# A convolution in products of 32 by 32 and an attention with the values stationary, in a four-layer network

## What is computed

```python
x = x + channel_attention(group_norm(x))             # layer 0
y = bn(einsum('bchw,oc->bohw', x, pw_w)) + x          # layer 1
x = gelu(bn(dwconv13x13(y)) + bn(y * dw1))            # 13 x 13 taps for each channel by itself
t = to_tokens(x)                                      # (16, 256, 96)
t = t + attention(ln(t))      # layer 2: 6 heads of 16, the diagonal masked
t = t + experts(ln(t))
t = t + attention(ln(t))      # layer 3: causal
t = t + experts(ln(t))
```

## Time and profile before

| | us |
|---|---|
| median of 3 runs | 1096.71 (1093.14 to 1098.74) |
| the profiled execution: time, span | 1101.9, 1100.2 |
| PE, PEld busy | 933.0, 819.4 |
| DVE, ACT, POOL busy | 605.9, 437.1, 371.5 |

### The profile page before, as it was taken

One profiled execution on the slowest core, in us unless ns is written; L12 is line 12 of the kernel. 1 busy time (PEld: TensorE's weight loads), 2 busy tenths in 40 slices (PEclk: granted clock), 3 DMA queues, 4 the chain that ended last, 5 costly groups with the idle time before them and its releaser, 6 DMA issues. The chain is left out here.

```text
span 1100.2 us, 19693 instructions
## 1 busy us (share of the span) xinstructions
PE 933.0 (85%) x6512; PEld 819.4 (74%) x6512; DVE 605.9 (55%) x1745; ACT 437.1 (40%) x698; POOL 371.5 (34%) x391
## 2 busy tenths in 40 slices
PE   2877778589854999999699999758899997999998
PEld 1655556378843988998699999747888886888887
DVE  5766566349454567775245565336667643443442
ACT  1343334320032443344255555313433424554553
POOL 3223333289030243212333343322342224324432
PEclk9986887679966999999799999957999997999999
DMA  3730000000005333340000000033434400000000
GB/s 73 120 39 0 0 0 0 1 1 0 0 12 119 66 66 79 78 91 10 1 1 0 0 0 0 1 86 81 93 73 92 94 1 0 9 7 14 7 7 15
DMA packets 27561, 36.75 MB, mean 33 GB/s; under 512 B 9288, under 2 KB 24448, under 8 KB 27520
## 3 DMA queue, kind: packets, MB, share of 16 engines
q1 hardware_dynamic: 27520, 36.24, 16.3%
HBM read 25.06 MB, written 11.17 MB: 33 GB/s over the span
## 5 line engine op out<-in xcount | busy, mean ns | idle before, releaser
L1427 PE MATMUL ps<-w,ff_b_h 128*128 128x96 f32 x1536 | 181.8, 275 | 6.7 <-ACT ff_b_fT L1483 6.7
L1427 PEld LDWEIGHTS ps<-w,ff_b_h 128*128 128x128 f32 x1536 | 178.5, 192 | 10.6 <-issue 7.3
L1494 ACT ACTIVATE ff_b_h<-ps,b 128x512 f32<-128x512 f32 x192 | 128.7, 687 | 122.5 <-PE ps L1419 122.3
L1030 PE MATMUL ps<-values,at_b_pT 128*128 128x102 f32 x1344 | 162.4, 277 | 1.0 <-POOL at_b_pT L955 0.4
L1030 PEld LDWEIGHTS ps<-values,at_b_pT 128*128 128x128 f32 x1344 | 156.0, 193 | 3.4 <-issue 1.5
L955 POOL TENSOR_SCALAR_AFFINE_SELECT at_b_pT<-at_b_pT 128x768 f32<-128x768 f32 x64 | 54.8, 868 | 237.9 <-ACT at_b_pT L1140 237.2
L1567 DVE SCALAR_TENSOR_TENSOR tok<-ps,ff_b_gate,tok 128x96 f32 (+1 forms) x224 | 56.0, 311 | 137.9 <-PE ps L1427 137.9
L1203 DVE TENSOR_REDUCE at_b_mf<-ps 128x6 f32<-128x1536 f32 (+1 forms) x64 | 98.1, 1553 | 25.5 <-PE ps L1007 24.9
L628 DVE SCALAR_TENSOR_TENSOR ca_qk<-ca_raw,dw,ca_qk 96x225 f32<-96x225 f32 (+1 forms) x256 | 98.8, 451 | 0.0
L1140 ACT ACTIVATE at_b_pT<-ps 128x1536 f32<-128x1536 f32 x64 | 80.9, 1291 | 43.3 <-PE ps L1015 43.1
L1005 PE MATMUL ps<-keys,at_b_qs 96*128 96x256 bf16 (+1 forms) x384 | 71.4, 274 | 22.4 <-issue 20.4
(11 more groups left out here) (228 smaller groups left out, 1605.0 us busy)
## 6 DMA issues: line engine op xcount, KB each, us to landing
at_parts<-at_b_part SPq DMA_DIRECT2D x96, 96.0 KB
at_b_qs<-at_parts SPq DMA_DIRECT2D x16, 288.0 KB, 4.2
keys<-at_parts SPq DMA_DIRECT2D x16, 288.0 KB, 5.3
at_b_qs<-at_parts SPq DMA_DIRECT2D x16, 192.0 KB, 5.8
keys<-at_parts SPq DMA_DIRECT2D x16, 192.0 KB, 6.3
w<-in_L_ffn_w SPq DMA_DIRECT2D x4, 576.0 KB
chan<-in_x SPq DMA_DIRECT2D x4, 384.0 KB, 5.1
at_b_qs<-at_parts SPq DMA_DIRECT2D x16, 96.0 KB, 6.5
```

What stands on the lines that cost most here:

```text
L1030: ins = nc.tensor.matmul(ps[:, 6 + u, OW * t:OW * (t + 1)], pT[:, u, k, h, P * t:P * (t + 1)], vp[:, slot, u, k, h, :], start=(n == 0), st ...
L1427: ins = nc.tensor.matmul(ps[:, 6 + e % 2, C * t:C * (t + 1)], h[:, e % 2, j, P * t:P * (t + 1)], f.w2[:, e * HC + j, :], start=(j == 0), s ...
L1494: nc.scalar.activation(h[:, e % 2, j, :], ps[:, 3 * (e % 2) + j, :], ACT.Gelu, bias=f.b1[:, e * HC + j:e * HC + j + 1]).then_inc(s_h, 1)
```

## The change

The convolution keeps its 16 x 16 bands, but takes two channels (PAIR = 32 partitions) at a time, since a 128 x 128 block diagonal matrix is zero outside of them. A part is four groups g = 4 part + q. Product (q, r) of a part takes the partitions 32 r to 32 r + 31 of group g as rows and writes partitions 32 q to 32 q + 31 of bank r: 16 products for each tap, one for each 32 x 32 block of the array. Banks 4 to 7 and 0 to 3 take turns by part. The loops are written out. All weights (`m.wt`, now [128, 12, 13, 32]) are made by POOL.

In the attention, the values of a head and 16 ones (VB = 32 columns) are now the weights, and the probabilities move: 256 columns for heads 0 to 3, on four column groups, into partitions 32 h to 32 h + 31; heads 4 and 5 by two tiles of 128 columns, again on four column groups. The sums then stand with values on the partitions. ACT copies them to `at_b_uo` (`sums`), PE turns them (`spread`, three transposes), and `out` goes on as before.

```diff
-def spread_weights(eng, m, g, k):
+def spread_weights(pool, m, g):
...
                 for q in range(QUADS):
                     for e in range(2):
                         for part in range(G // QUADS):
...
+                link(pool.memset(m.mask[:, :], 0.0))
+                for q in range(QUADS):
+                    one = m.mask[PAIR * q:PAIR * (q + 1), :]
+                    link(pool.memset(one, 1.0))
...
-                for g in range(SLOTS):
-                    spread_weights(pool, m, g, g).then_inc(s_wp, 1)
+                for g in range(G):
+                    spread_weights(pool, m, g).then_inc(s_wp, 1)
                     pool.wait_ge(s_wp, g + 1)
...
-                pe.wait_ge(s_cin, G // 2)
-                pe.wait_ge(s_wp, SLOTS)
-                pe.sem_inc(s_wd, SLOTS)
-                with pe.Fori(0, G // SLOTS) as i:
-                    for k in range(SLOTS):
-                        pe.wait_ge(s_wd, i * SLOTS + k + 1)
-                        pe.wait_ge(s_gl, i * SLOTS + 1)
-                        order = [R] + [j for j in range(KW) if j != R]
-                        for n, j in enumerate(order):
-                            y0, y1 = max(0, R - j), HH - max(0, j - R)
-                            ins = nc.tensor.matmul(
-                                ps[:, 4 + k, 0:B * HH].rearrange("p (b y) -> p b y", y=HH)[:, :, y0:y1],
-                                m.wt[:, k, j, :],
-                                cin[:, bass.ds(i * SLOTS + k, 1), :, y0 + j - R:y1 + j - R].rearrange("p g b y -> p (g b) y"),
-                                start=(n == 0), stop=(n == KW - 1))
-                        ins.then_inc(s_cv, 1)
+                def convolve(part):
+
+                    pe.wait_ge(s_wp, QUADS * (part + 1))
+                    pe.wait_ge(s_cin, 2 * (part + 1) if part % 2 == 0 else G // 2)
+                    if part >= 2:
+                        pe.wait_ge(s_gl, QUADS * (part - 1))
+                    order = [R] + [j for j in range(KW) if j != R]
+                    for n, j in enumerate(order):
+                        y0, y1 = max(0, R - j), HH - max(0, j - R)
+                        for q in range(QUADS):
+                            g = QUADS * part + q
+                            for r in range(QUADS):
+                                rows_in = slice(PAIR * r, PAIR * (r + 1))
+                                out = ps[PAIR * q:PAIR * (q + 1), (4 + 4 * part + r) % 8, 0:B * HH].rearrange("p (b y) -> p b y", y=HH)
+                                ins = nc.tensor.matmul(out[:, :, y0:y1], m.wt[rows_in, g, j, :],
+                                                       cin[rows_in, g, :, y0 + j - R:y1 + j - R],
+                                                       start=(n == 0), stop=(n == KW - 1), skip_group_check=True)
+                                if n == KW - 1:
+                                    ins.then_inc(s_cv, 1)
...
-                for g in range(SLOTS, G):
-                    dve.wait_ge(s_cv, g - SLOTS + 1)
-                    spread_weights(nc.vector, m, g, g % SLOTS).then_inc(s_wd, 1)
...
-                def weighted_values(i, slot, u, t):
-                    if t == 0:
-                        pe.wait_ge(s_zero, 4 * i + 2 * u + 2)
-                    terms = [(k, h) for k in range(1 if causal and t == 0 else TPI) for h in range(H)]
-                    for n, (k, h) in enumerate(terms):
-                        ins = nc.tensor.matmul(ps[:, 6 + u, OW * t:OW * (t + 1)], pT[:, u, k, h, P * t:P * (t + 1)],
-                                               vp[:, slot, u, k, h, :], start=(n == 0), stop=(n == len(terms) - 1))
-                    if t == TPI - 1:
-                        ins.then_inc(s_O, 1)
+                def weighted_values(i, slot, u, k):
+
+                    pe.wait_ge(s_zero, 4 * i + 2 * u + k + 1)
+                    n0 = P if causal and k == 1 else 0
+                    for h in range(4):
+                        nc.tensor.matmul(ps[VB * h:VB * (h + 1), 6 + u, n0:N], vp[:, slot, u, k, h, :], pT[:, u, k, h, n0:N],
+                                         start=(k == 0), stop=(k == TPI - 1), skip_group_check=True)
+                    for t in range(n0 // P, TPI):
+                        for h in range(4, H):
+                            q = 2 * t + h - 4
+                            ins = nc.tensor.matmul(ps[VB * q:VB * (q + 1), 6 + u, N:N + P], vp[:, slot, u, k, h, :],
+                                                   pT[:, u, k, h, P * t:P * (t + 1)], start=False,
+                                                   stop=(k == TPI - 1 or (causal and t == 0)), skip_group_check=True)
+                    if k == TPI - 1:
+                        ins.then_inc(s_U, 1)
+
+                def spread(i, u):
+
+                    pe.wait_ge(s_uc, 2 * i + u + 1)
+                    w = OB // TPI
+                    for t in range(TPI):
+                        nc.tensor.transpose(ps[:, 6 + u, w * t:w * t + P], uo[:, u, P * t:P * (t + 1)], m.ident[:, :])
+                    nc.tensor.transpose(ps[:, 6 + u, 0:OB].rearrange("p (t n) -> p t n", t=TPI)[:, :, P:w],
+                                        uo[:, u, N:N + P], m.ident[:, :]).then_inc(s_O, 1)
...
+                def sums(i, u):
+                    act.wait_ge(s_U, 2 * i + u + 1)
+                    nc.scalar.copy(uo[:, u, :], ps[:, 6 + u, 0:OB]).then_inc(s_uc, 1)
```

## The result

The changed kernel takes 1063.62 us (median of 4 runs, 1058.86 to 1068.01) against 1097.72 for the kernel before: ratio 0.9692, 95% interval 0.9633 to 0.975. The forecast was 1130 and on the wrong side. The profiled execution took 1065.9 us with a span of 1064.2.

The account below looks back on a forecast made before the run. PE was taken to pace the convolution, a DVE and ACT chain to run beside it in the attentions. 51 - 2 + 0.4 - 21 + 4 = +32 on 1101.9 gives 1134, by the median 1130; own range 1115 to 1165, whole range 1038 to 1180.

Parts of the forecast that it names:

- One product costs one pass time: 624 x 0.176 = 110 us: Convolution: a product's second pass holds up the next block, so 110 us against 59.3, +51 us; chance 0.45.
- Rival (a): All passes overlap, issue rate decides: convolution about 50 us, attention rounds gain 1.8 and 2.2, total 1052; chance 0.35.
- Conv's start at 234: Convolution: starts at 234 instead of 236, since weights spread by POOL are there before the columns, -2 us.
- POOL's twelve steps: Convolution: POOL spreads weights from 32 columns instead of 128, a quarter of 11.88 / 3 us each, four some 4 us.
- The 24 back copies: Convolution: 24 copies of 128 columns instead of 12 of 256, 5.8 against 5.4 us, +0.4.
- The attention's -21: Both token attentions: seven steady rounds each give -12.6 us, layer ends -4.7 and -3.5, together -21 us.
- -0.7 and -1.1: Attention rounds: 0.7 us shorter a round, 1.1 in the causal layer, -12.6 us over seven steady rounds each.
- Ends shorter by 4.7 and 3.5: Attention layers' ends, where nothing overlaps: -4.7 us, and -3.5 in the causal layer.
- Drains, +4: Attention: changing how the array is cut drains it, six changes a round, 96 in all: +4 us, bounds 0 and 9.

Follow-up runs that it names:

- `taps_inner`: The changed kernel with the convolution's 624 products reordered, 13 taps of one array block behind each other, then the next block: 1409.2 us in one run, convolution 370 us.
- `after2`: The changed kernel again, unedited, measured beside another run: 0.9685 of the kernel before (0.9657 to 0.9712).
- `warm3`: The changed kernel with throwaway products in three idle places of each attention round (ten over 512 columns, twice ten of 128): 0.9574 of the kernel before (0.9519 to 0.963).

## Why the prediction was wrong

**Failed: "One product costs one pass time: 624 x 0.176 = 110 us".** The step assumed that PE starts its matmuls in program order, so that a product's second pass holds up the next block. It doesn't: the stretch is 33.9 us (32.0 to 34.3 in the other runs with these products in this order), 54 ns a product. With the 110 in place of 34 the sum was 76 us too high, more than the whole miss of 68 (1134 for 1065.9 on the profiled execution); the attention, 16 us short of its term, hid a part. `taps_inner` shows the reverse case, where successive passes do share a place.

**Rival (a) had the mechanism**, "the rate of issue decides", with 36 to 72 us. The measured 34 lies just under its lower end; what sets it is not a time per pass but the arrival of code, which the forecast named only as something that could make it wrong. Rival (a)'s 1052 was missed by the attention: (a) took the block at 0.7 to 0.9 us, which is right (0.86), and gains of 1.8 and 2.2 us a round, where the changed kernel's rounds at full clock gain 1.2.

**The small terms.** "Conv's start at 234": it began at 230.5, but in the other runs with the new convolution anywhere from 227.6 to 235.6, so not all of this is the change. POOL's twelve steps took 14.13 us, 1.2 each where a quarter of 4.0 was forecast, and the first four were there when the columns were. The 24 back copies take 5.47 us (forecast 5.8).

**The attention's -21.** The rounds' chain did get shorter, by more than forecast in layer 2, and the term's size in the changed kernel was wrong because of the clock. Rounds: forecast -0.7 and -1.1; the full-clock rounds are 22.4 against 23.55 and, in `after2`, 19.7 against 20.9, -1.2 in both; the mean over the steady rounds is +0.2 and +1.2, in `after2` -0.1 and +0.5. "Ends shorter by 4.7 and 3.5": 5.2 and 2.8 behind the last copies, beside 3.6 and 1.0 in the last rounds, which the forecast counted as steady. With the idle places filled the attention's part comes to -21.6 us (746.4 us from the first copy of the maxima to the end before, 724.8 in `warm3`), with the clock as it stands -4.6, or -11.2 in `after2`. The forecast's sentence "if the granted clock … fell" named a falling clock, gave it no term and no chance, and tied it to few blocks at work; here it fell in rounds that leave PE idle. That -21.6 is close to -21 is partly luck: the rounds gained more than forecast, the places were filled by products the change doesn't have, and the drains are in it.

**Drains, +4.** The cost is there and can be read from the starts of a block:

```profile
409.77 0.22 PE L1015 MATMUL ps<-diag_b,ident_b 128*128 128x128 bf16 x1
409.92 0.64 PE L1038 MATMUL ps<-at_b_pT,values 128*32 128x256 f32 x8
...
410.71 0.69 PE L1067 MATMUL ps<-wT,outT 97*128 97x96 f32 x4
```

Into a block, a start comes 0.15 us after that of a bf16 product of 128 columns, where before it came 0.055 after it. Out of it, the next product starts 0.20 us after the block's last one, where 128 fp32 columns take 0.11 and where before it was 0.11 too. So a change of cut costs about 0.09 us on PE, the same in most blocks; 96 changes make some 9 us of PE's time (an estimate), a third of the forecast's upper bound of 26. How much of it lies on the chain isn't shown, since the round's measured gain holds it already. The Trainium skill (TensorEngine Tiling (Array Packing), Key Properties) has such a drain, and these starts agree with it.

## What to carry to other kernels

Small products on different places of the array overlap if neighbours in the program use different places; then count instructions, since straight code came in at 256 per 3.7 us here, and a product that saves array time may be bound by that. When a change makes TensorE idle in a round that others bound, read the granted clock of each round: the gain may be there and be eaten by it, and filling the idle time, with moved work or even with throwaway products, gave it back here. Judge it by rounds at full clock beside the mean.

## What the runs showed of the hardware

- Second passes of fp32 products on 16 places start after the first passes of all 16, out of program order, 6 to 7 ns between starts. This convolution signals on each place's last product; whether one signal on the last product in the program would be enough, no run shows.
- Only about four waiting passes of one place are let past: with 26 in a row on one place, 22 of them run alone (370 us for 1248 passes).
- A TensorE that is busy 100% of 360 us on one block of sixteen, two at the seams, is granted 0.50.
- A change between products on the whole width of the array and products on 32 of its columns costs about 0.09 us each way.
- Straight code on TensorE: 128 passes of 32 by 32 (256 instructions, a packet of 16 KB) every 3.5 to 4.0 us, whatever their columns; out of a loop, 128 in 2.5 to 2.6 us.
